# Moving start-up work and four FFN pieces in a one-core attention + mixture-of-experts kernel

## The reference, cut to what matters

```python
# x (32, 256, 256), ctx (32, 77, 256), all float32
def xattn(q, k, v, W, b, mask):            # 16 heads of 16
    scores = einsum(qh, kh) / sqrt(16)      # causal and padding mask -> -inf
    out = einsum(softmax(scores), vh)
    return out @ W.T + b
def ffn(x, w_in, w_out, w1, w2, wg, we, gb, eb):
    shared = swiglu(x @ w_in.T) @ w_out.T   # hidden 512
    # 2 groups of 4 experts: best group, top 2 experts in it, softmax weights
    h = swiglu(x @ w1.T)
    routed = sum_e (h * w_se[:, e]) @ w2[e].T
    return shared + routed
x = x + tanh(g_xattn) * xattn(layernorm(x), ctx, ctx, W, b, mask)
x = x + tanh(g_ffn) * ffn(layernorm(x), ...)
```

## Time and profile before

| | |
|---|---|
| three runs | 1168.62, 1170.35, 1170.63 us |
| median | 1170.35 us |
| the profiled execution | 1171.33 us, of which its span 1169.6 us |
| mean granted TensorE clock | 0.990 |
| busy: PE, DVE, POOL, ACT | 1108.6, 814.3, 523.0, 473.3 us |

### The profile page before, as it was taken

One profiled execution on the slowest core, in us unless ns is written; L12 is line 12 of the kernel. 1 busy time (PEld: TensorE's weight loads), 2 busy tenths in 40 slices (PEclk: granted clock), 3 DMA queues, 4 the chain that ended last, 5 costly groups with the idle time before them and its releaser, 6 DMA issues.

```text
span 1169.6 us, 22483 instructions
## 1 busy us (share of the span) xinstructions
PE 1108.6 (95%) x7475; PEld 917.9 (78%) x7475; DVE 814.3 (70%) x1778; ACT 473.3 (40%) x723; POOL 523.0 (45%) x647
## 2 busy tenths in 40 slices
PE   4878999999999999999999899999999899999997
PEld 2556878888887788788787677788888788888886
DVE  6567687686785786776867676557545488777776
ACT  4545555555545555555555442223222111111111
POOL 5333456447447347356446422200000566666564
PEclk9989999999999999999999999999999899999999
DMA  8984657647647556665753411478653444554452
GB/s 148 224 143 119 127 94 148 135 112 121 137 111 111 128 122 100 142 123 104 138 126 84 94 37 46 172 241 260 214 190 110 157 159 144 170 164 151 151 168 72
DMA packets 106163, 160.65 MB, mean 137 GB/s; under 512 B 28828, under 2 KB 70718, under 8 KB 106048
## 3 DMA queue, kind: packets, MB, share of 16 engines
q1 hardware_dynamic: 94276, 121.18, 45.6%
q0 software_dynamic: 11776, 38.03, 10.4%
HBM read 75.24 MB, written 52.10 MB: 109 GB/s over the span
## 4 chain that ended last, share of the span: by engine, by line
PE 69%; DVE 11%; issue 9%; POOL 7%; ACT 2%; DMA 0%; POOLq 0%; ACTq 0%; DVEq 0%
PE ps L746 15%; PE ps L793 12%; PE ps L691 7%; PE ps L795 6%; PE ps L708 6%; PE ps L611 3%; PE ps L599 3%; PE ps L642 3%; PE ps L778 3%; POOL tab_dram L1457 3%; PE ps L567 2%; PE ps L571 2%; PE ps L665 1%; PE ps L594 1%; PE ps L676 1%
## 5 line engine op out<-in xcount | busy, mean ns | idle before, releaser
L793 PE MATMUL ps<-regr,gh 128*128 x600 | 221.7, 407 | 0.1
L875 ACT ACTIVATE Pt<-ps,pbias 77x1024 f32<-77x1024 f32 x128 | 141.4, 1105 | 115.2 <-PE ps L599 111.0
L795 PE MATMUL ps<-regr,gl 128*128 x600 | 170.0, 283 | 0.0
L793 PEld LDWEIGHTS ps<-regr,gh 128*128 128x128 f32 x600 | 113.8, 190 | 23.9 <-issue 0.5
L965 ACT ACTIVATE gh<-ps 128x512 fp32r<-128x512 f32 x75 | 44.9, 598 | 204.9 <-PE ps L778 123.4
L1175 DVE TENSOR_REDUCE mneg<-ps 128x8 f32<-128x616 f32 x128 | 100.6, 792 | 20.5 <-PE ps L571 20.5
L795 PEld LDWEIGHTS ps<-regr,gl 128*128 128x128 f32 x600 | 114.0, 190 | 0.0
L691 PE MATMUL ps<-x2h,winh 128*128 128x512 f32 x256 | 109.8, 429 | 0.5 <-DVE OHR L1080 0.5
L1358 POOL TENSOR_TENSOR gl<-gf,gh 128x512 fp32r<-128x512 f32 x64 | 82.4, 1288 | 47.8 <-ACT gh L832 47.6
L1433 POOL TENSOR_TENSOR x<-x,regf 128x512 f32<-128x512 f32 x32 | 41.6, 1301 | 133.0 <-DMA x<-in_x 133.0
L691 PE MATMUL ps<-x2h,winl 128*128 128x512 f32 x256 | 101.0, 395 | 0.0
(11 more groups left out here) (202 smaller groups left out, 2740.0 us busy)
## 6 DMA issues: line engine op xcount, KB each, us to landing
regr<-regr SPq DMA_DIRECT2D x96, 256.0 KB, 6.2
y_dram<-Pt SPq DMA_DIRECT2D x64, 256.0 KB, 2.2
regf<-in_x SPq DMA_DIRECT2D x32, 256.0 KB, 2.9
x<-in_x SPq DMA_DIRECT2D x32, 256.0 KB, 7.2
y_dram<-res SPq DMA_DIRECT2D x32, 256.0 KB
regr<-regr SPq DMA_DIRECT2D x96, 77.0 KB, 6.9
x_dram<-x2h SPq DMA_DIRECT2D x14, 512.0 KB, 3.0
x_dram<-x2l SPq DMA_DIRECT2D x14, 512.0 KB, 3.8
```

Source lines behind the costliest of these rows:

```text
L793: e.matmul(o, gh2[:, k % 3, fc, :], w2v[:, bass.ds(val, 1), fc, :, :].rearrange("p o h d -> p (o h) d"), start=fc == 0, stop=False, skip_g ...
L795: m = e.matmul(o[:, 0, :], gl2[:, k % 3, fc, :], w2v[:, bass.ds(val, 1), fc, 0, :].rearrange("p o d -> p (o d)"), start=False, stop=fc == ...
L875: e.activation(Pt[0:K, 4 * k:4 * k + 4, :].rearrange("k (n j) t -> k n (j t)", n=2), bank_of["sc", b, k][0:K, :, :], ACT.Exp, bias=pbias[: ...
```

## The change

Six edits:

1. At the start, DVE no longer clears `Kbd`, and ACT no longer copies it into `Kst`. DVE clears bank 0 of `Kst` itself, behind `klo` of the first keys. POOL's first `keys` waits for one thing less.
2. `own` of bank 1 moves on ACT from slot 5 of iteration 1 (ahead of `xT` of batch 1) to slot 8 (behind it).
3. The zeros of bank 1 move on DVE from slot 10 of iteration 1 (ahead of the maxima of batch 1) to slot 4 of iteration 2 (behind them); the six DMAs that fill bank 1 move with them on SP.
4. The low half `winl` moves on DVE from iteration 4, slot 9, to iteration 5, slot 2; `wol` from iteration 5, slot 9, to iteration 6, slot 1. Their high halves on ACT stay.
5. The first tanh of the FFN waits for three low halves and not four.
6. Near the end of the FFN, pieces 0 to 3 of chunk 15 are put ahead of pieces 19 to 23 of chunk 14. The routing entries keep their positions in the list.

```diff
--- before.py
+++ after.py
@@ -36,7 +36,7 @@
 DCON = {n: i + 1 for i, n in enumerate(
-    "idb kb0 m8 va_zero va_one ones rec pre_zero pre wgh0 lb0 tgh brow pbias crow kcol ks1".split())}
+    "idb m8 ks0 va_zero va_one ones rec pre_zero pre wgh0 lb0 tgh brow pbias crow kcol ks1".split())}
 GCON = {n: i + 7 for i, n in enumerate("ident caus cauT upb kint fold foldb".split())}
@@ -64,9 +64,14 @@
     held = len(ROUTES) - 2
     logits = set()
+
+    pieces = list(range(24 * NCH))
+    cut = 24 * (NCH - 2) + 19
+    pieces[cut:cut + 9] = pieces[cut + 5:cut + 9] + pieces[cut:cut + 5]
+
     def ffn(routes):
-        order.append(("ffn", at["ffn"] // 24, at["ffn"] % 24))
+        order.append(("ffn", pieces[at["ffn"]] // 24, pieces[at["ffn"]] % 24))
         at["ffn"] += 1
         for _ in range(routes):
             route()
@@ -114,10 +119,11 @@
             slots[9].append(("own", 0, 0))
             slots[11].append(("load_kv", 1, 0))
         if i == 1:
-            slots[5].append(("own", 1, 0))
-            slots[10] += [("gates", 0, 0), ("zeros", 0, 0)]
+            slots[8].append(("own", 1, 0))
+            slots[10].append(("gates", 0, 0))
             slots[11].append(("masks", 1, 0))
         if i == 2:
+            slots[4].append(("zeros", 0, 0))
             slots[6].append(("pads", 1, 0))
             slots[11].append(("load_weights", 0, 0))
@@ -126,6 +132,11 @@
             slots[10].append(("weights", 1, 0))
         if i in (4, 5):
             slots[9].append(("weights", i - 2, 0))
+
+        if i == 5:
+            slots[2].append(("weights_low", 2, 0))
+        if i == 6:
+            slots[1].append(("weights_low", 3, 0))
         if i % 2 == 1 and i + 1 < NB:
             slots[11] += [("kv", i // 2 + 1, 0), ("vau", i // 2 + 1, 0)]
         if i % 2 == 0 and 0 < i < NB - 2:
@@ -191,7 +202,7 @@
             "xT mm mTp sc val O aT pj x2T lg lgt ha hb so rank T1 T2 T3 ga gb tz ex "
-            "tg khi xn xTh mT P ks0 ks1 OT aTh x2h lgT t gh re1 re2 sh wh t2 gh2 "
+            "tg khi xn xTh mT P ks1 OT aTh x2h lgT t gh re1 re2 sh wh t2 gh2 "
             "dcon klo mom0 mom1 xTl pad mx mhi mlo rden att aTl x1 n2 x2l LG u f res sl rv rdif rsub rcc roh rslot rrec "
             "nt en tk ti ei wl u2 f2 gl2 acc0 acc1 "
@@ -412,6 +423,15 @@
                 e.dma_start(vf[:, :, :], A["ctx_1024"][b * G:b * G + G].rearrange("b k d -> k b d")).then_inc(
                     s[f"vf{h}"], 16)
+            def spread_kv(b):
+
+                h = b % 2
+                for r, t in enumerate((khi, klo, khi)):
+                    for j in range(2):
+                        o = 32 * r + 16 * j
+                        dst = Kst[o:o + 16, h, j, :, :, :].rearrange("p q a k -> p (q a k)")
+                        e.dma_start(dst.bitcast(F), t[64 * j:64 * j + 64, :, :].bitcast(F)).then_inc(s[f"kd{h}"], 16)
+
             for stage_, b, k in order:
                 h = b % 2
                 if stage_ == "load_x":
@@ -446,19 +466,18 @@
                     e.dma_start(wout_s, A["woutT"].rearrange("(c p) n -> p c n", p=P)).then_inc(s["w1"], 16)
                 elif stage_ == "load_kv":
                     load_kv(b)
-                elif stage_ == "kv":
+                elif stage_ == "kv" and b != 1:
                     e.wait_ge(s["klo"], b + 1)
                     if b == 0:
-                        e.wait_ge(s["ks0"], 1)
-                    if b == 1:
-                        e.wait_ge(s["dcon"], DCON["ks1"])
+                        e.wait_ge(s["dcon"], DCON["ks0"])
                     if b >= 2:
                         e.wait_ge(s["sc"], 4 * G * (b - 1))
-                    for r, t in enumerate((khi, klo, khi)):
-                        for j in range(2):
-                            o = 32 * r + 16 * j
-                            dst = Kst[o:o + 16, h, j, :, :, :].rearrange("p q a k -> p (q a k)")
-                            e.dma_start(dst.bitcast(F), t[64 * j:64 * j + 64, :, :].bitcast(F)).then_inc(s[f"kd{h}"], 16)
+                    spread_kv(b)
+                elif stage_ == "zeros":
+
+                    e.wait_ge(s["klo"], 2)
+                    e.wait_ge(s["dcon"], DCON["ks1"])
+                    spread_kv(1)
                 elif stage_ == "queries":
                     e.wait_ge(s["xTl"], b + 1)
                     if b >= 2:
@@ -582,8 +601,10 @@
                 elif stage_ == "scores":
                     if k == 0:
                         if b == 0:
+                            e.wait_ge(s["ks1"], 1)
+                            e.wait_ge(s["gcon"], GCON["cauT"])
+                        if b == G:
                             e.wait_ge(s["ks1"], 2)
-                            e.wait_ge(s["gcon"], GCON["cauT"])
                         e.wait_ge(s[f"kd{ks}"], 96 * (b // G // 2 + 1))
                         e.wait_ge(s[f"xs{h}"], 48 * (b // 2 + 1))
                         e.wait_ge(s[f"mt{h}"], 16 * (b // 2 + 1))
@@ -839,11 +860,6 @@
                         e.wait_ge(s["kbd"], 2 * G * b)
                         e.wait_ge(s[f"kd{1 - h}"], 96 * ((b - 1) // 2 + 1))
                     e.activation(khi[:, :, :], kf[:, :, :], ACT.Copy).then_inc(s["khi"], 1)
-                    if b == 0:
-
-                        e.wait_ge(s["dcon"], DCON["kb0"])
-                        e.activation(Kst[0:96, 0, :, :, :, :].rearrange("r j q a k -> r (j q a k)"),
-                                     Kbd[0:96, :, :, :, :].rearrange("p g c q k -> p (g c q k)").bitcast(F), ACT.Copy).then_inc(s["ks0"], 1)
                 elif stage_ == "norm":
                     e.wait_ge(s["nm"], b + 1)
                     if b >= 1:
@@ -910,7 +926,7 @@
                         n = 4 * b + fc
                         e.wait_ge(s["ha"], n + 1)
                         if n == 0:
-                            e.wait_ge(s["sl"], 4)
+                            e.wait_ge(s["sl"], 3)
                         if n >= 2:
                             e.wait_ge(s["f"], n - 1)
                         e.activation(tt[:, n % 2, :], bank_of["ha", b, fc][:, :], ACT.Tanh, scale=0.5).then_inc(s["t"], 1)
@@ -1121,7 +1137,6 @@
             nonlocal_count = [0]
             e.wait_ge(s["gcon"], GCON["ident"])
             e.tensor_copy(identb[:, :], ident[:, :]).then_inc(s["dcon"], 1)
-            e.memset(Kbd[:, :, :, :, :].bitcast(F), 0.0).then_inc(s["dcon"], 1)
             e.tensor_reduce(own8[:, :], ident[:, :].rearrange("p (j d q) -> p j q d", j=2, q=4), AX, ALU.add).then_inc(s["dcon"], 1)
             routing = None
@@ -1131,6 +1146,8 @@
                 if stage_ == "kv":
                     e.wait_ge(s["khi"], b + 1)
                     e.tensor_tensor(klo[:, :, :], kf[:, :, :], khi[:, :, :].bitcast(F), ALU.subtract).then_inc(s["klo"], 1)
+                    if b == 0:
+                        e.memset(Kst[0:96, 0, :, :, :, :].bitcast(F), 0.0).then_inc(s["dcon"], 1)
                 elif stage_ == "init":
                     e.memset(Vau[:, :, :, :, :], 0.0).then_inc(s["dcon"], 1)
                     e.wait_ge(s["dcon"], DCON["va_zero"])
@@ -1252,7 +1269,7 @@
                     if k == 0:
                         routing = route(b)
                     next(routing, None)
-                elif stage_ == "weights":
+                elif (stage_ == "weights" and b < 2) or stage_ == "weights_low":
                     e.wait_ge(s["sh"], b + 1)
                     if b == 2:
                         for c in range(2):
```

## The result

| | before | changed | ratio, 95% interval |
|---|---|---|---|
| first comparison, medians | 1170.49 us | 1160.72 us (1156.3 to 1162.64, 4 runs) | 0.9916, 0.9892 to 0.9941 |
| the same kernel again, second session | 1171.08 | 1163.81 (1161.86 to 1169.52, 6 runs) | 0.9927, 0.9901 to 0.9954 |
| and a third time | 1173.7 | 1164.9 (1158.56 to 1171.53, 11 runs) | 0.9930, 0.9904 to 0.9957 |

The gains between medians are 9.8, 7.3 and 8.8 us; 7.7 were forecast.

What follows compares the result with a forecast made beforehand. TensorE's work in fixed order was taken to bound the kernel from about 100 us on, chains of waits before that. 2.8 + 1.9 + 1.0 + 0.5 + 1.5 = 7.7 us off gave 1163.0 us, range 1159.5 to 1168.0.

Steps and rivals of the forecast that it cites:

- The start: Batch 1's maxima start at about 23.6 us, not 26.87; less 0.4 for batch 0's maxima, gain 2.8 us (1.0 to 4.4).
- the front: Program start: DVE's first moments start some 0.7 us sooner without the early clear; 0.3 us of it carried on.
- winl: TensorE's 4.00 us wait before 79.31 us: `x2l` starts 1.9 us sooner, 2.1 us of wait remain; ends 0.9 and 1.9.
- The clock there: From 80 to 90 us, granted clock 0.72 behind TensorE's 4.00 us wait; a shorter wait gains 1.0 us (0 to 2.6).
- wol: Moving it removes TensorE's 0.81 us wait at 103.72 us; gain 0.5 us, between 0.8 gained and 1.2 lost.
- a new wait on the maxima behind `wol`: Sign of being wrong: TensorE newly waits between 100 and 120 us on the maxima behind the moved `wol`.
- The FFN's end: TensorE's 2.54 us wait for GpSimd is replaced by 1.6 us on `rank`; gain 1.5 us (0.3 to 2.4).
- The root: Rival, program start: the memset behind the first `klo` holds GpSimd's root; gain 7.7 - 1.5, 1164.5 us; chance 0.15.
- The loads: Rival: DMA arrivals pace the front, losing the 2.8 and part of 1.9; gain 4.0, 1167.0 us; chance 0.12.
- The clock holding everywhere: Rival: no clock fall at 79 and 720 us and an earlier rise at the start; 1160 us; chance 0.13.
- the slower case: Rival: the rank wait and thinner stretches leave TensorE at 1.2 GHz for long; 1173 us; chance 0.03.
- the wait at batch 4: Sign of being right: TensorE's wait before batch 4's third maximum is about 2 us.

Runs made afterwards that it cites:

- winl_only: The kernel before with only the low half `winl` moved behind the maxima, `wol` left in its old place: 1167.55 us, ratio 0.9965 (0.9945 to 0.9985).
- own_only: The kernel before with only bank 1's ownership rows moved behind the high half of batch 1's transpose: 1168.81 us, ratio 0.9993 (0.9971 to 1.0015).

## Why the prediction was right

**The sum.** 7.7 us were forecast, and 9.8, 7.3 and 8.8 measured; 1160.72 lies in the range, 2.3 below the forecast. Timed alone in one session, edits 1 to 3, 4 and 5, and 6 gave 4.1, 4.1 and 0.8 us between medians. The places and what ends the waits there were right. That the sum came so near is in part luck, since the sizes erred both ways: the start gave some 0.8 more than its term, `wol` 0.4 more at a full clock, the clock behind `winl` 1.0 less, and edit 6 itself 0.8 less.

**The start, 2.8 us.** The mechanism was right: the maxima of batch 1 start at 23.37, where near 24 was forecast. The size was 0.7 to 1.0 short. The 0.4 us taken off for batch 0's maxima was not needed: ACT's small copy ahead of batch 1 (L884, L868 before) starts 0.2 us sooner (18.55 to 18.32). And the 0.3 us that the front was to carry on is not in the term: 26.87 - 23.6 - 0.4 is 2.8 or 2.9, and 3.2 with it. Edit 2's own share is 1.1 in place of 1.8; the clears give 2.5 and not 2.1, since the idle 0.46 us ahead of the memset goes with it.

**winl, 1.9 us.** Right: 2.04 us of wait remain in the three executions that reach it at a full clock (the changed kernel's second and third, and `winl_only`). The 2.5 us of `winl` fit the hole behind the maxima.

**The clock there, 1.0 us.** Not given. The granted clock in the window from 60 to 110 us, before and then changed:

```profile
60.00:110.00 50.00, 39.74 (x296) 30.52 (x296) 32.69 (x63) 27.30 (x38) 18.29 (x25) 0.90 0.70 148
```

```profile
60.00:110.00 50.00, 45.41 (x331) 34.71 (x330) 32.41 (x71) 29.16 (x42) 20.06 (x32) 0.86 0.59 134
```

It is 0.86 again in the second execution and 0.93 in the third. With the wait shortened or gone, the clock still fell somewhere in this part.

**wol, 0.5 us.** Right in sign, and 0.4 too small at a full clock: 0.64 and 0.81 us of wait go and 0.56 come back, 0.9 in all. The term knew only the 0.81, since the larger wait was hidden in the trace before. The 0.56 is one of the prediction's own signs of being wrong, a new wait on the maxima behind `wol` (at 97.44, 102.41 and 97.82 us in the three executions, where 100 to 120 was named); it was too short to turn the term. `klo` fell only to 1.39 us, because it still meets GpSimd's residual instruction. The rule of the Trainium skill (SBUF — State Buffer, Who interferes with whom), by which 0.8 us would have been lost, did not bear here: `wol` took its 1.22 us with GpSimd idle.

**The FFN's end, 1.5 us.** The wait was replaced as worked out, by 1.79 to 1.98 us on `rank` where 1.6 was forecast. Against the trace of before, the gain is 0.6 where the clock falls (1.0 was forecast) and 1.9 to 2.1 where it does not (2.4): the wait was 0.2 to 0.4 longer. But the 1.4 us between the two forecasts was the clock's, and `own_only` got 1.3 of it without the edit. The edit's own worth was 1.0 by the prediction's sum and is 0.6 to 0.8 by the traces.

**The rivals.** The root is 0.72 us beside the clear, so the first falls. The loads did not pace the front: batch 1's maxima and the third of batch 4 are ended by ACT and DVE. The clock holding everywhere happened in none of the three executions. TensorE never stayed at 1.2 GHz long enough for the slower case. By its own signs the prediction was right but for the 0.56 us above and for the wait at batch 4, which is 2 us only where TensorE reaches it at a full clock. What no case had is the spread: executions of one program differ by 5 us at 115 us.

## What to carry to other kernels

Look for work that nobody awaits yet ahead of the instruction that TensorE waits for. Measure what moving it gives from a nearby instruction ahead of it and not from the start of the program, so that an unrelated delay in one trace does not hide the gain. A wait read behind a stretch at a low clock can be shorter than it is at a full one. Compare only stretches with the same granted clock before a difference is put down to an edit. When a wait is replaced, work out the new one as well and put as much work ahead of it as it is long. Before making a late transfer early, look at what its reader will then run beside; an idle wait on one engine can be what keeps another one fast.
